# Moving the quantised product of a finished tile, and its scaling, to later places in a step

## The reference

```python
q, k, v = x_norm @ Wq, x_norm @ Wk, x_norm @ Wv      # 32 query heads, 8 key/value heads of 64
q, k = apply_rope(q, pos), apply_rope(k, pos)
scores = where(causal, q @ k.T / 8, min)
x = x + (softmax(scores) @ v) @ Wo                   # attention and residual
h = layernorm(x)                                     # per token
scale = max(absmax(h), 1e-7) / 127
qh = clip(round(h / scale), -128, 127)               # int8 per token
x = x + float16(qh @ weight.T * scale * w_scale + bias)
```

## Time and profile before

| | |
|---|---|
| time, median of 3 runs | 793.66 us (791.88 to 794.1) |
| the profiled execution | 792.76 us, span from first to last instruction 791.0 us |
| busy in the span | PE 743.3, PEld 647.6, DVE 636.3, ACT 623.8, POOL 570.5 us |
| mean granted TensorE clock | 0.988 of full speed |

### The profile page before, as it was taken

How to read it: one execution, slowest core, us unless ns; L and a number is a source line. 1 busy time by engine, 2 the same in 40 slices (tenths; PEclk the granted TensorE clock), 3 DMA queues, 4 the chain that set the end, 5 groups by cost and what they waited for, 6 DMA issues and landing times.

```text
span 791.0 us, 23157 instructions
## 1 busy us (share of the span) xinstructions
PE 743.3 (94%) x7974; PEld 647.6 (82%) x7974; DVE 636.3 (80%) x1648; ACT 623.8 (79%) x1734; POOL 570.5 (72%) x524
## 2 busy tenths in 40 slices
PE   4799999999999999999999999999999999999893
PEld 3587888888888888888888888988888888888772
DVE  5757888787888888888778888888788888887887
ACT  4578888788778888888778878887888778887873
POOL 4376878787876887877886898778787797686402
PEclk9899999999999999999999999999999999999996
DMA  8254555564554554555544455455444555454300
GB/s 265 58 126 95 128 121 136 125 152 112 134 121 99 118 122 107 125 118 120 129 105 117 116 130 119 106 131 127 111 108 113 128 128 118 92 118 99 94 2 27
DMA packets 56994, 90.97 MB, mean 115 GB/s; under 512 B 12592, under 2 KB 19248, under 8 KB 56880
## 3 DMA queue, kind: packets, MB, share of 16 engines
q1 hardware_dynamic: 53808, 79.02, 43.6%
q0 software_dynamic: 3072, 10.49, 5.2%
HBM read 16.06 MB, written 2.10 MB: 23 GB/s over the span
## 4 chain that ended last, share of the span: by engine, by line
PE 68%; ACT 11%; DVE 9%; issue 6%; DMA 2%; SPq 2%; POOL 0%; ACTq 0%; POOLq 0%; DVEq 0%
PE x_bank L623 21%; PE t_bank L740 15%; PE o_bank L756 11%; ACT prob L1035 8%; PE s_bank L719 7%; PE s_bank L720 6%; PE ot_bank L807 3%; DVE probT L1364 3%; PE t_bank L623 2%; DVE neg_max L1376 2%; PE s_bank L725 2%; DMA qT<-wv 1%; DVE o_norm L1407 1%; SPq L305 1%; DMA prob<-in_w_value 1%
## 5 line engine op out<-in xcount | busy, mean ns | idle before, releaser
L1035 ACT ACTIVATE prob<-s_bank,neg_max 128x384 f32<-128x384 f32 (+3 forms) x512 | 267.2, 533 | 62.4 <-DVE neg_max L1384 32.9
L1364 DVE SCALAR_TENSOR_TENSOR probT<-t_bank,probT 128x512 f16<-128x512 f32 x320 | 215.9, 683 | 28.2 <-ACT probT L1048 27.3
L1048 ACT ACTIVATE probT<-t_bank 128x512 f16<-128x512 f32 x320 | 189.1, 603 | 38.0 <-PE t_bank L740 35.6
L740 PE MATMUL t_bank<-ident,prob 128*128 128x128 f32 x1280 | 198.7, 278 | 6.7 <-ACT prob L1035 3.9
L719 PE MATMUL s_bank<-kT,qT 128*128 128x384 f32 (+3 forms) x512 | 176.0, 359 | 7.1 <-ACT prob L1035 6.0
L493 POOL TENSOR_TENSOR wv<-raw,wv 128x512 fp32r<-128x512 f32 x62 | 79.5, 1282 | 118.9 <-ACT wv L996 118.9
L740 PEld LDWEIGHTS t_bank<-ident,prob 128*128 128x128 f32 x1280 | 142.6, 141 | 27.6 <-ACT prob L1035 11.9
L1384 DVE CUSTOM_DVE_ANT_0 s_bank<-s_bank,mask_row 128x512 f32<-128x512 f32 (+1 forms) x256 | 156.2, 642 | 3.9 <-PE s_bank L720 0.3
L720 PE MATMUL s_bank<-kT,qT 128*128 128x384 f32 (+3 forms) x512 | 156.6, 321 | 0.0
L756 PE MATMUL o_bank<-value,probT 128*128 128x64 f16 x3840 | 138.4, 193 | 0.0
L756 PEld LDWEIGHTS o_bank<-value,probT 128*128 128x128 f16 x3840 | 131.4, 98 | 6.0
(11 more groups left out here) (125 smaller groups left out, 994.4 us busy)
## 6 DMA issues: line engine op xcount, KB each, us to landing
qT<-wv SPq DMA_DIRECT2D x248, 128.0 KB, 2.4
swp<-raw SPq DMA_DIRECT2D x320, 64.0 KB, 2.1
kT<-key_pair SPq DMA_DIRECT2D x128, 128.0 KB, 2.4
wg_raw<-in_w_group POOLq DMA_DIRECT2D x16, 384.0 KB, 4.9
wg_raw<-in_w_group POOLq DMA_DIRECT2D x16, 256.0 KB, 3.8
resid<-in_x SPq DMA_DIRECT2D x4, 512.0 KB, 8.4
out<-resid SPq DMA_DIRECT2D x16, 128.0 KB, 2.0
wo_stage<-in_w_out SPq DMA_DIRECT2D x4, 256.0 KB, 3.5
```

Source lines behind the costliest of these rows:

```text
L740: last = nc.tensor.transpose(t_bank[B % TURN_BANKS][:, h * P:(h + 1) * P], prob[:, B % PROBS, h, :], ident[:, :])
L1035: nc.scalar.activation(prob[:, slot:slot + blocks, h, :], s_bank[G % SCORE_BANKS][:, at * n:(at + 1) * n].rearrange("p (k n) -> p k n", n= ...
L1048: nc.scalar.activation(turned_half[B % TURNED][HI], t_bank[B % TURN_BANKS][:, :], ACT.Copy, scale=PROB_SCALE).then_inc(probT_hi, 1)
L1364: nc.vector.scalar_tensor_tensor(out=turned_half[B % TURNED][LO], in0=t_bank[B % TURN_BANKS][:, :], scalar=PROB_SCALE, in1=turned_half[B % ...
```

## The change

On TensorE `ffn_product` moves from behind `scores(s, 8)` to between `attend(s, 2)` and `attend(s, 3)`. On VectorE `scale_product` moves from behind `maxima(s, 8)` to behind `normalise_output(s, 1)`. For the first tile a wait for the load of the scale rows is added, which was issued in step 8. No instruction is added or taken away.

```diff
                 turn(s, 3)
                 scores(s, 8)
-                ffn_product(done_tile(s))
                 scores(s, 9)
                 turn_output(s, 0)
...
                 attend(s, 1)
                 attend(s, 2)
+                ffn_product(done_tile(s))
                 attend(s, 3)
                 attend(s, 4)
                 turn(s, 6)
...
+                if f == 0:
+                    dve.wait_ge(rows_loaded, 32)
                 dve.wait_ge(ffn_done, f + 1)
...
                 maxima(s, 8)
-                scale_product(done_tile(s))
                 keep_probT_low(s, 3)
...
                 normalise_output(s, 1)
+                scale_product(done_tile(s))
                 batch_statistics(s, 3)
                 keep_probT_low(s, 5)
```

## The result

The changed kernel takes 797.94 us in the median of 4 runs (796.97 to 798.6), the kernel before 793.25 us beside it. The ratio is 1.0056 with a 95% interval of 1.0038 to 1.0075: slower by a little over half a percent, 4.7 us (3.0 to 6.0 us by the interval). The profiled execution of the changed kernel took 797.81 us with a span of 796.0 us, 5.0 us longer than the span before.

A forecast was written before the change was run, and what follows sets the result against it. TensorE was taken to bound the kernel. A net 0.84 - 0.50 = 0.34 us in 11 steps (3.7 us) plus about 1.0 us in step 30 made 4.7 us, forecasting 798.4 us, range 796 to 800.5.

The forecast's parts named there:

- gain up to the end of the attention product of block 4: TensorE, per ordinary step: between 0.42 and 0.55 us gained from the waits that go, taken as 0.50.
- product's matmuls at the new place: L796 between the attention products: the two matmuls keep today's price, about 0.23 us, so no difference in ordinary steps.
- output product of part 0 behind the inversion's start: TensorE waits for the scaling behind the normalisation of part 1, starting at 498.69 instead of 497.70, 0.99 us later.
- step 30, net: Step without projection, idling for ScalarE at `turn(s, 5)`: 0.23 - 0.10 + 0.84, about 1.0 us slower.
- The removed wait: TensorE at the product L796, waiting for VectorE's clipping L1464: 0.49 us that goes.
- the second one behind it: Projection L623 waiting for the scaling L1472 to release the product's bank: a hidden 0.06 us that goes too.
- The new wait: Output product of part 0 waits for `product_scaled`: 0.99 us later per step, bounds 0.91 to 1.05.
- the shift at `turn(s, 8)`: `turn(s, 8)` waits for ScalarE's last exponential, behind `keep_oT`: 0.84 us later than before, none given back.
- A (given back): Rival, between `turn(s, 8)` and the next scores: delay returned before the step ends; 788.3 us, chance 0.05.
- B (short release, hidden matmuls): Rival, no change: short release saves 1.0 us, product's matmuls vanish between attention products, 2.8 us; 794.6 us, chance 0.10.
- C (TensorE carried by the full 0.99): Rival, blocks 7 to 9: ScalarE and VectorE, shifted 0.99 us, carry TensorE along; 1.8 us more, 800.2 us, chance 0.20.
- D (late transfers of queries): Rival: query transfers land in another order and a step waits for them; total would pass 802 us, chance 0.05.

## Why the prediction was right, point by point

Forecast 798.4 us, measured 797.94. The forecast of the difference, 4.7 us, agrees with the medians more closely than their interval of 3.0 to 6.0 us can tell, and that is chance. What carries the verdict is that the terms come out one by one in the timelines. In step 19:

| term | predicted | measured |
|---|---|---|
| gain up to the end of the attention product of block 4 | 0.50 | 0.49 (inversion from 8.19 to 7.70 us into the step) |
| product's matmuls at the new place | about 0.23 | 0.21 |
| output product of part 0 behind the inversion's start | 0.19 + 0.99 = 1.18 | 1.18 |
| wait of `turn(s, 7)` that goes with it | 0.18 | 0.19 |
| net, to the output product of part 1 | +0.34 | +0.35 (8.88 + 2.60 against 8.38 + 2.75) |
| step 30, net | +1.0 | +0.94 (8.88 + 2.60 against 7.80 + 2.74) |
| sum | 4.7 | 5.0 by the starts in all 12 steps, 4.7 by the medians |

**The removed wait** went as said, with the second one behind it. Of the 0.55 us, 0.49 are left behind the attention products. The prediction had laid the missing 0.05 to `turn(s, 5)`, and it is there: that turn starts 5.39 us into the step (496.23), 0.05 us behind the end of its exponential, and the attention products follow 0.50 us behind it (496.73) instead of 0.43 (495.48 to 495.91). The experiment that moved the product alone shows that the two waits are one chain: a wait that goes without its partner comes back 1.4 us later. The prediction had this as a hidden 0.06 us at the projection, and the size was right, but the two are listed there as separate gains of 0.49 and 0.06, and in a step with a projection the first can't be had without the second.

**The new wait** is what the prediction named, in place and size. Its position on VectorE's list sets it: three places for the scaling gave stretches of 7.89, 8.40 and 9.48 us beside the changed kernel's 8.88, each within 0.02 us of what was expected from the rows of the changed kernel. The prediction had idle time of some 0.9 us in the row; the row has 0.74, because it counts from the modelled end of `turn(s, 6)`. Start to start, the output product is 1.38 us behind `turn(s, 6)` instead of 0.39, the 0.99 of the sum.

**Step 30.** There the removed wait of 0.49 us brought only 0.12. The same wait for ScalarE stands ahead of `turn(s, 5)` as in the earlier trace rows, 0.67 us long instead of 0.65. Before, with the opening output product and those of parts 0 and 1, and now:

```profile
737.62 0.97 PE L623 MATMUL x_bank<-wo,oT 128*128 128x256 f32 x6
...
745.41 0.96 PE L623 MATMUL x_bank<-wo,oT 128*128 128x256 f32 x6
...
748.16 0.95 PE L623 MATMUL x_bank<-wo,oT 128*128 128x256 f32 x6
```

```profile
741.78 0.97 PE L623 MATMUL x_bank<-wo,oT 128*128 128x256 f32 x6
...
745.63 0.39 PE L719 MATMUL s_bank<-kT,qT 128*128 128x256 f32 x1 [0.30 <-ACT prob L1035]
...
747.17 0.65 PE L740 MATMUL t_bank<-ident,prob 128*128 128x128 f32 x4 [0.67 <-ACT prob L1035]
...
750.66 0.95 PE L623 MATMUL x_bank<-wo,oT 128*128 128x256 f32 x6 [0.74 <-DVE value L1474]
```

`turn(s, 5)` starts 5.39 us into the step (747.17 - 741.78), before 5.51 (743.13 - 737.62). This is the "up to 0.1" that the prediction let come through ScalarE. The kernel with the product alone moved has the gain too (a stretch of 7.67 us in step 30, 7.80 before), since no projection waits for the scaling there. A second wait, 0.30 us at score group 10, wasn't foreseen. It costs nothing, since the larger one stands behind it.

**ScalarE** was to set the shift at `turn(s, 8)`. Its last exponential of the step:

```profile
500.92 0.47 ACT L1061 ACTIVATE oT<-ot_bank,pow_rows 128x256 fp32r<-128x256 f32 x1 [0.85 <-PE ot_bank L807]
501.29 0.47 ACT L1035 ACTIVATE prob<-s_bank,neg_max 128x256 f32<-128x256 f32 x1
501.65 0.20 ACT L1035 ACTIVATION_READ_ACCUMULATOR prob<-s_bank,neg_max 128x1 f32 x1
```

It ends at 501.85, and `turn(s, 8)` starts at 501.90, so TensorE is just released by it. But blocks 7 to 9 then follow at TensorE's pace.

**The rivals.** A (given back): from the output product of part 1 to that of part 3 step 19 takes 11.77 us (502.32 to 514.09), 11.76 before, and over the 12 steps the sums are equal to 0.1 us, so nothing is given back. The kernel with the scaling one place later says the same for a longer delay. B (short release, hidden matmuls): the release was the long one, 0.15 us, the matmuls cost 0.21. C (TensorE carried by the full 0.99): the stretch to the output product of part 1 is 0.15 us shorter, as in the forecast. D (late transfers of queries): the changed kernel's profile has no wait of TensorE for such a transfer.

**Held instructions.** The prediction took from the Trainium skill, "VectorE: DVE Perf Modes", section "Two Vector instructions with no wait between them", that the scaling isn't held. The trace agrees: the scaling started 0.34 us behind the start of the normalisation, before its end at 0.42. What a held one would cost isn't shown here.

## What to carry to other kernels

Ask of every moved instruction where its consumer's release comes from: the reader of a shared bank belongs into the last idle time of its engine ahead of the next user of that bank. Here 0.5 us of idle stood two instructions in front of the chosen place, and those two places are 9.6 us apart in a kernel of 793. When a wait is removed, look for the next instruction that waits for the same chain, since it may only hand the wait on. And where an instruction has two waits, the one that is satisfied last should be the one it carries itself.

## What the runs showed of the hardware

The order in which two waits are written was worth 0.07 and 0.09 us at the two places where it was swapped, both where TensorE really waits: the release took 0.05 to 0.06 us when the weight load carried the wait, 0.14 to 0.15 us when a wait instruction stood ahead of it. At `turn(s, 7)` this adds up to 2.1 us over 32 steps, by the starts in the timelines.

A single profile can be off by more than the effect studied. The profiled execution of the kernel with the product alone moved took 797.89 us, though the median is 794.81. One wait for the queries' transfer stands out, in step 3, where its program is that of the kernel before (PE):

```profile
146.47 0.30 PE L719 MATMUL s_bank<-kT,qT 128*128 128x128 f32 x1 [1.42 <-DMA qT<-wv]
```

The kernel before has three such waits of at most 0.3 us in the whole profile, the changed one none. Why a transfer was late there stays open. The late transfer cost twice. From the output product of part 1 to that of part 3 this step 3 takes 14.81 us, in the changed kernel 11.74, so 3.07 us more, and only about half of it is the wait. Behind the wait TensorE first works at full clock and then slower. The profile's view of two stretches of it, with the granted clock as the third number from the end (PE, PEld, DVE, ACT and POOL busy ahead of it):

```profile
146.50:147.60 1.10, 1.10 (x9) 1.00 (x10) 0.00 (x0) 0.00 (x0) 0.96 (x2) 1.00 0.93 317
148.80:150.60 1.80, 1.80 (x8) 1.46 (x6) 0.85 (x3) 1.25 (x8) 0.00 (x0) 0.50 0.53 129
```

The granted clock is 1.00 in the first (2.4 GHz) and 0.50 in the second (1.2 GHz), after TensorE had stood idle for 1.42 us. From the first attention product behind the wait to the scores behind the next output product it takes 3.97 us (147.62 to 151.59), in the changed kernel 2.48, so 1.5 us more, with the low clock in it. Waits of 0.37 and 0.56 us at the same place, in the kernels with the scaling ahead of the inversion and one instruction later, were not followed by a lower clock.

Lengths from the opening output product of a step to those of parts 0 and 1 repeated to 0.04 us all the same, in steps 10 to 31 where the kernels have the same lists there, and the comparisons above rest on those.
